# Routing of a mixture of experts: token places listed on chip during the routing stage, results stored at fixed rows and gathered by place

## The chip, the cores and the metric

The kernel runs on one core of a Trainium2 chip. The time is the device time of one launch, in microseconds (us), from the first to the last instruction with what lies around it. Three runs of the kernel before gave 2531.51, 2540.93 and 2547.09 us; the median is 2540.93.

## The reference, cut to what matters

A decoder layer on x [8, 100, 1024]: self attention, cross attention over 722 context rows, and a mixture of 64 experts of which each token takes 8. The change is in the third part, where B = 8 batches of S = 100 tokens make 800 tokens and 6400 (token, expert) pairs:

```python
router_logits = x2d @ gate_w                                  # [800, 64]
routing_weights = softmax(router_logits)
routing_weights, selected_experts = top_k(routing_weights, 8)
routing_weights = routing_weights / sum(routing_weights)
flat_sel = selected_experts.reshape(-1)
sorted_sel = argsort(flat_sel); token_idx = sorted_sel // 8
sorted_inputs = take(x2d, token_idx)                          # rows, expert by expert, bf16
w0 = ragged_dot(sorted_inputs, gate); w1 = ragged_dot(sorted_inputs, up)   # 1024 -> 384
expert_out = ragged_dot(silu(w0) * w1, down)                  # 384 -> 1024
out[t] = sum_k weight[t, k] * expert_out[row of (t, k)]
```

## The kernel before, in words

`decoder_kernel` runs seven stages one after the other: `self_attention_phase`, `query_phase`, `cross_image_phase`, `cross_text_phase`, `route_phase`, `experts_phase` and `combine_phase`. Each stage is a block: its engines run their own instruction lists, ordered by semaphores, and no engine begins the next stage until all have ended this one. So a stage lasts as long as its slowest engine list, waits for its own DMAs included.

**Casting ahead.** `Precast` copies the experts' f32 weights to bf16 in DRAM, 192 transfers on POOL's queue, two in flight, spread over the first four stages.

**Blanking.** In `self_attention_phase` POOL's list ends with 72 such casts and then 19 transfers of 1.5 MB of zeros over the rows of `results_d` (L242), one at a time: each waits for the one before to land, and the list ends with a wait for the last. Results that no tile of an expert ever writes are zeros by this. The other engines' work ends with the output projection: PE (L83), DVE's sum with the residual (L350), SP's store of x1 (L219).

**Routing stage** (`route_phase`). Per batch b PE projects the attention output (two halves of 24 matmuls, L81 to L83), DVE adds x1 (L1646), takes statistics and writes the normed rows `xn` (L1664), PE turns them (L1739) and multiplies by the gate (L1745), ACT copies out the logits (L1704). PE's order is project(b+1), router(b). POOL adds the bias to x1 (L1614) and stores `xn` as bf16 rows in DRAM (L1620). At the end SP waits for the casts and loads the first three experts' weights.

**Experts stage** (`experts_phase`). It starts with the choice of experts for all batches at once on DVE (`route`, L2004 to L2033: exp, top 8, marks, places from two matmuls), a table of tile counts and starts (`tabulate`), and for each expert a comparison of [100, 8 x 256] places with the marks (`seat_rows`, L2087) whose result PE multiplies by token numbers (`number_rows`, L2224, 32 matmuls of one column): this gives the numbers of the expert's tokens, which DVE casts to an index (L2101) and POOL uses to gather 128 rows of 2 KB (L1951). Then, in a loop over the 64 experts unrolled by four, step e of PE is: turn the rows of e+1 (L2245), the products of e with gate and up (L2253, 48 matmuls), the narrow product of e-1 (L2261), the numbers for e+4 (L2224). Experts with over 128 tokens run `further`: a tile more of the whole sequence with nothing beside it (L2293, L2253, L2261). The tile's indices come with the first gather; only a third tile needs new ones. Weights are held in four slots; SP loads e+3 (2304 KB, L1929) once the narrow product of e-1 has freed the slot. ACT stores results of 128 rows (256 KB, L2192) at a row that it loads from the table (`first_tile`). In the last steps DVE works out each token's result rows and weights (`find_results`, `find_weights`, `order_weights`, L2056 to L2083).

**Combining stage** (`combine_phase`). POOL gathers, for each batch and each of 8 choices, 100 rows of 2 KB by index (L2358, 64 gathers); DVE (5 of 8) and PE (3 of 8) weigh and add them.

Of the kernel before, what the change touches and what calls it, by code (L numbers as in the profile page):

```python
# [85 lines left out]
def self_attention_phase(nc, sems, cast, x_d, w_d, x1_d, clear_d):  # L86
# [9 lines left out]
    CLEARS = 19  # L96
    X_SLOTS, R_SLOTS = 4, 4
    with ExitStack() as ctx:
# [4 lines left out]
        zeros = sc.sb("zeros", [P, D], BF16)  # L103
# [38 lines left out]
        cleared, made, blanked = sc.sem("cleared"), sc.sem("made"), sc.sem("blanked")  # L142
# [81 lines left out]
        def _(pool):  # L224
# [7 lines left out]
            pool.memset(zeros[:, :], 0.0).then_inc(cleared, 1)  # L232
# [3 lines left out]

            blank = clear_d.rearrange("(c n p) d -> c p n d", p=P, c=CLEARS)
            pool.wait_ge(cleared, 3)
            for c in range(CLEARS):

                wait(pool, blanked, 16 * c)
                pool.dma_start(blank[c], zeros[:, :].unsqueeze(1).broadcast_to(blank[c].shape)  # L242
                               ).then_inc(blanked, 16)
            pool.wait_ge(blanked, 16 * CLEARS)

# [1261 lines left out]
MAX_TILES = ROWS // P + EXPERTS  # L1507
MATS, MAT = 3, KT * FF


class Routing:


    def __init__(self, sc):
        self.x2 = sc.sb("x2", [S, B, D])
        self.logits = sc.sb("logits", [S, B, EXPERTS])
        self.weights = sc.sb("weights", [S, B, TOP_K])
        self.results = sc.sb("results", [S, B * TOP_K], I32)


        self.table = sc.sb("table", [1, 4, EXPERTS], I32)

# [5 lines left out]
TILES, FIRST, FURTHER, THIRD = range(4)  # L1528


def route_phase(nc, sems, r, cast, x1_d, attn_d, w_out_d, b_out_d, gate_d, xn_d):

    with ExitStack() as ctx:
# [8 lines left out]
        at_raw = sc.sb("at_raw", [P, 2, KT, S])  # L1542
# [7 lines left out]
        std = sc.sb("std", [S, 2])  # L1550
        outp = sc.ps("outp", [P, 2, BANK])
        turn = sc.ps("turn", [P, 2, BANK])
        logit_ps = sc.ps("logit_ps", [P, BANK])

# [8 lines left out]
        outp_ready, x2_ready, x2_seen = sc.sem("outp_ready"), sc.sem("x2_ready"), sc.sem("x2_seen")  # L1563
        stats_done, stats_seen, var_ready = sc.sem("stats_done"), sc.sem("stats_seen"), sc.sem("var_ready")
        std_ready, rstd_ready, xn_ready = sc.sem("std_ready"), sc.sem("rstd_ready"), sc.sem("xn_ready")
        sent, send_step = [sc.sem(f"sent{u}") for u in range(2)], sc.sem("send_step")
        turned, xnT_ready = sc.sem("turned"), sc.sem("xnT_ready")
        router_ready, logits_ready = sc.sem("router_ready"), sc.sem("logits_ready")
        block = ctx.enter_context(nc.Block())

        @block.sync
        def _(sp):
# [34 lines left out]
        def _(pool):  # L1607
# [20 lines left out]
            for u in range(2):  # L1628
                send(B - 2 + u, u)
# [896 lines left out]
```

## Time and profile before

| | |
|---|---|
| median of 3 runs | 2540.93 us (2531.51 to 2547.09) |
| profiled execution, span | 2527.7 us (it is given as a span alone; its own time is not shown) |
| PE busy | 2011.5 us, 80% |
| PE weight load busy | 1692.7 us, 67% |
| DVE busy | 1130.7 us, 45% |
| ACT busy | 646.6 us, 26% |
| POOL busy | 468.2 us, 19% |
| DMA | 518.81 MB, mean 205 GB/s |

The spans of the stages, by the first instruction of each: self attention 0 to 510.7, queries to 672.7, cross attention to 1677.4, routing to 1827.9, experts to 2423.0, combining to the end. A slice of the page's busy table is 63.2 us. "Idle before, released by" names what ended an engine's wait; "issue" is a wait for nothing that the profile shows, such as a branch or a fetch of instructions.

### The profile page before, as it was taken

What the parts mean: (1) busy time and instruction counts of PE and PEld (TensorE: products, weight loads), DVE (VectorE), ACT (ScalarE), POOL (GpSimd) and SP (SyncE); (2) the same over time, 40 slices, a digit from 0 to 9 for tenths busy, and PEclk for the clock granted to TensorE, in tenths of its full rate; (3) what the DMA queues carried; (4) which work ended last, traced back from release to release, by engine and by line L of the source; (5) the groups of instructions that cost most, each with busy time, mean ns of one, the idle gap of its engine ahead of it and who ended that gap; (6) DMA issues with size and microseconds to landing.
All of it is one profiled execution on the core that took longest, in us unless ns stands there. A gap on an engine that the chain in (4) does not pass through costs nothing. (4 is left out here: it accounts for less than half of the span.)

```text
span 2527.7 us, 48690 instructions
## 1 busy us (share of the span) xinstructions
PE 2011.5 (80%) x17744; PEld 1692.7 (67%) x17745; DVE 1130.7 (45%) x2122; ACT 646.6 (26%) x1391; POOL 468.2 (19%) x556
## 2 busy tenths in 40 slices
PE   5999886059298989999959899959857788877756
PEld 4999864037298978888758777736656666666622
DVE  4444510034233354444433566643365555554366
ACT  4333300033221234434321344431101111111112
POOL 0111101101000011111100111101133334332156
PEclk9999988569699989999979999979979999999965
DMA  7999997669987255555276587833459989898445
GB/s 183 214 215 222 218 239 253 235 187 228 268 215 159 78 121 137 121 129 129 66 190 162 150 198 184 191 108 81 163 181 366 353 314 416 335 373 343 176 147 161
DMA packets 148152, 518.81 MB, mean 205 GB/s; under 512 B 27154, under 2 KB 68114, under 8 KB 140858
## 3 DMA queue, kind: packets, MB, share of 16 engines
q0 software_dynamic: 31776, 215.85, 38.2%
q1 hardware_dynamic: 105162, 281.04, 30.7%
q10 hardware_dynamic: 11088, 20.19, 2.1%
q8 instruction: 84, 1.38, 0.2%
q14 instruction: 42, 0.34, 0.0%
HBM read 582.94 MB, written 236.06 MB: 324 GB/s over the span
## 5 line engine op out<-in xcount | busy, mean ns | idle before, releaser
L81 PE MATMUL img_acc<-img_ctx_hi,img_w_hi 128*128 128x258 f32 x1024 | 303.4, 296 | 51.4 <-DVE img_ctx_lo L1158 40.1
L82 PE MATMUL img_acc<-img_ctx_lo,img_w_hi 128*128 128x258 f32 x1024 | 295.0, 288 | 0.1
L83 PE MATMUL img_acc<-img_ctx_hi,img_w_lo 128*128 128x258 f32 x1024 | 294.7, 288 | 0.0
L1780 POOL DMA_DIRECT2D experts_bf_dram<-in_moe_dram x192 | 98.3, 512 | 871.7 <-DMA experts_bf_dram<-in_moe_dram 542.2
L81 PEld LDWEIGHTS img_acc<-img_ctx_hi,img_w_hi 128*128 128x128 f32 x1024 | 199.8, 195 | 76.1 <-issue 65.4
L1951 POOL DMA_INDIRECT moe_rows<-expert_rows_dram,moe_index x77 | 150.3, 1952 | 387.1 <-DVE moe_index L2101 382.6
L82 PEld LDWEIGHTS img_acc<-img_ctx_lo,img_w_hi 128*128 128x128 f32 x1024 | 199.9, 195 | 0.4 <-issue 0.4
L83 PEld LDWEIGHTS img_acc<-img_ctx_hi,img_w_lo 128*128 128x128 f32 x1024 | 200.0, 195 | 0.0
L81 PE MATMUL txt_acc<-txt_ctx_hi,txt_w_hi 128*128 128x320 f32 x512 | 169.5, 331 | 37.5 <-DVE txt_ctx_lo L1158 29.2
L82 PE MATMUL txt_acc<-txt_ctx_lo,txt_w_hi 128*128 128x320 f32 x512 | 161.8, 316 | 0.0
L83 PE MATMUL txt_acc<-txt_ctx_hi,txt_w_lo 128*128 128x320 f32 x512 | 161.7, 316 | 0.0
L2087 DVE TENSOR_TENSOR moe_seated<-moe_picked,moe_seat 100x2048 bf16<-100x2048 f32 x64 | 145.9, 2282 | 0.1
L81 PE MATMUL self_acc<-self_xnT_hi,self_w_hi 128*128 128x400 f32 x384 | 136.6, 356 | 2.1 <-DVE self_xnT_lo L271 2.1
L81 PEld LDWEIGHTS txt_acc<-txt_ctx_hi,txt_w_hi 128*128 128x128 f32 x512 | 99.2, 194 | 52.1 <-issue 39.1
L82 PE MATMUL self_acc<-self_xnT_lo,self_w_hi 128*128 128x400 f32 x384 | 133.1, 347 | 0.0
L83 PE MATMUL self_acc<-self_xnT_hi,self_w_lo 128*128 128x400 f32 x384 | 132.6, 345 | 0.0
L83 PEld LDWEIGHTS txt_acc<-txt_ctx_hi,txt_w_lo 128*128 128x128 f32 x512 | 99.6, 194 | 0.0
L82 PEld LDWEIGHTS txt_acc<-txt_ctx_lo,txt_w_hi 128*128 128x128 f32 x512 | 99.4, 194 | 0.0
L2423 PE MATMUL comb_acc<-comb_part,comb_diag 100*100 100x512 bf16 x144 | 60.9, 592 | 43.6 <-DMA comb_part<-expert_results_dram,routing_results 41.5
L1045 POOL TENSOR_TENSOR img_kT<-img_kT,img_norm 128x258 f32<-128x258 f32 x64 | 47.0, 735 | 258.7 <-DMA img_kT<-cross_k_dram 258.6
L2245 PE MATMUL moe_turn<-moe_ident,moe_rows 128*128 128x128 bf16 x512 | 45.7, 233 | 60.6 <-issue 30.8
L745 PE MATMUL query_x_turn<-query_ident,query_xn 100*128 100x100 f32 x64 | 8.2, 281 | 104.1 <-ACT query_xn L705 101.6
(321 smaller groups left out, 4332.9 us busy)
## 6 DMA issues: line engine op xcount, KB each, us to landing
experts_bf_dram<-in_moe_dram POOLq DMA_DIRECT2D x192, 768.0 KB, 8.5
routing_w<-experts_bf_dram SPq DMA_DIRECT2D x48, 2304.0 KB
moe_w_last<-experts_bf_dram SPq DMA_DIRECT2D x16, 2304.0 KB
expert_results_dram<-self_zeros POOLq DMA_DIRECT2D x19, 1536.0 KB
self_w_raw<-in_w_self_dram SPq DMA_DIRECT2D x32, 512.0 KB, 12.0
expert_results_dram<-moe_out ACTq DMA_DIRECT2D x64, 256.0 KB, 7.3
img_raw<-in_ctx_img_dram SPq DMA_DIRECT2D x8, 1032.0 KB, 6.3
cross_k_dram<-img_kT SPq DMA_DIRECT2D x64, 129.0 KB, 2.0
```

The source lines that it names most:

```text
L81: eng.matmul(out, w_hi, a_hi, start=first, stop=False)
L82: eng.matmul(out, w_hi, a_lo, start=False, stop=False)
L83: return eng.matmul(out, w_lo, a_hi, start=False, stop=last)
L745: mm = pe.transpose(dst[:, kt // (KT // 2), col:col + S], src[:, kt * P:(kt + 1) * P], ident[0:S, 0:S])
L1045: pool.tensor_tensor(k, k, m.norm[:, cols:cols + part.cols], ALU.mult).then_inc(s.k_ready, 1)
L1780: pool.dma_start(self.dst_d[n], self.src_d[n]).then_inc(self.done[u], 16)
L1951: pool.indirect_dma_start(out=dst, out_offset=None, in_=xn_d[:, :], in_offset=bass.IndirectOffsetOnAxis(ap=rows_of, axis=0)).then_inc(load ...
L2087: return dve.tensor_tensor(dst, picked[:, :, bass.ts(e, 1)].broadcast_to(shape), seat[:, 0:places].unsqueeze(1).broadcast_to(shape), ALU.i ...
L2245: mm = pe.transpose(turn[:, k, :], rows[:, c % W_SLOTS, 0, k::KT], ident[:, :])
L2423: mm = pe.matmul(acc[0:S, b % 2, h, :], diag[:, done % 2, p, :], part[:, k, h * BANK:(h + 1) * BANK], start=n == 0 and p == 0, stop=k == O ...
```

## The change

The blanking goes, with its tile `zeros`. The experts stage no longer works out token numbers: `route`, `tabulate`, `seat_rows`, `number_rows`, `find_results` and `order_weights` are gone from it. In their place the routing stage does this per batch, on DVE, PE and POOL beside the projection: `choose` (top 8, their numbers, the marks), `rank` (two small matmuls), `find_places` (each token's 8 places, expert x 896 + rank), and `scatter` (POOL writes each token's number to its 8 places in DRAM lists, 4 bytes a token, 100 tokens an instruction, 8 instructions a batch, spread over four lists so that four are in flight). At the end SP loads the four lists, DVE takes their minimum, PE turns it, and `r.token` holds for every expert and tile the 128 token numbers. Unlisted places hold 800, a row of zeros. Results go to row e x 896 + 128 j, and the combining stage gathers by the places. The routing loops are unrolled, `at_raw` now shares memory with `at_lo`, and the results in DRAM are declared as 512 int32 a row instead of 1024 bf16.

```diff
 # self_attention_phase, POOL
-            pool.memset(zeros[:, :], 0.0).then_inc(cleared, 1)
             pool.wait_ge(x_split, B // 2)
             cast.start_some(pool, *CASTS_SELF)
-            blank = clear_d.rearrange("(c n p) d -> c p n d", p=P, c=CLEARS)
-            for c in range(CLEARS):
-                wait(pool, blanked, 16 * c)
-                pool.dma_start(blank[c], zeros[:, :]...).then_inc(blanked, 16)
-            pool.wait_ge(blanked, 16 * CLEARS)
 # route_phase, SP
-                wait(sp, at_split, b - 1)
+                wait(sp, outp_ready, 2 * (b - 1))
                 sp.dma_start(at_raw[:, u], attn_rows[b]).then_inc(at_loaded[u], 16)
...
+            sp.wait_ge(router_ready, B)
+            for n in range(LISTS):
+                sp.wait_ge(listed[n], 16 * B * TOP_K // LISTS)
+                sp.dma_start(list_rows[:, n], list_d[n].rearrange(...)).then_inc(list_loaded, 16)
+            sp.wait_ge(list_loaded, 16 * LISTS)
 # route_phase, POOL
+            def scatter(b):
+                pool.wait_ge(places_ready, b + 1)
+                for k in range(TOP_K):
+                    wait(pool, listed[k % LISTS], 16 * (b * TOP_K // LISTS + k // LISTS))
+                    pool.sem_inc(scatter_step, 1)
+                    pool.indirect_dma_start(
+                        out=list_d[k % LISTS][:, :],
+                        out_offset=bass.IndirectOffsetOnAxis(ap=r.places[:, b, k:k + 1], axis=0),
+                        in_=numbers[:, b:b + 1], in_offset=None).then_inc(listed[k % LISTS], 16)
+            for b in range(B):
+                send(b, b % 2)
+                if b + 2 < B:
+                    add_bias(b + 2, b % 2)
+                if b > 0:
+                    scatter(b - 1)
+            scatter(B - 1)
 # route_phase, DVE
+            def choose(b, u):
+                dve.wait_ge(logits_ready, b + 1)
+                link(dve.max(r.top[:, b, :], logits[:, u, :]))
+                dve.max_index(which[:, :], r.top[:, b, :], logits[:, u, :])
+                link(dve.match_replace(rest[:, :], r.top[:, b, :], logits[:, u, :], SELECTED))
+                dve.tensor_tensor(chosen[:, u, :], rest[:, :], logits[:, u, :],
+                                  ALU.not_equal).then_inc(chosen_ready, 1)
+                link(dve.tensor_tensor(match[:, :, :], expert_no..., which..., ALU.is_equal))
+            def find_places(b, u):
+                dve.wait_ge(ranked, b + 1)
+                link(dve.tensor_tensor(place[:, :], rank_ps[0:S, 0:EXPERTS], place_start[:, :], ALU.add))
+                link(dve.tensor_tensor(so_far[:, :], so_far[:, :], chosen[:, u, :], ALU.add))
+                link(dve.tensor_tensor(match[:, :, :], match[:, :, :], place..., ALU.mult))
+                link(dve.tensor_reduce(place_of[:, :], match[:, :, :], AX.X, ALU.add))
+                dve.tensor_copy(r.places[:, b, :], place_of[:, :]).then_inc(places_ready, 1)
+            for b in range(B):
+                norm(b, b % 2)
+                if b + 2 < B:
+                    split_at(b + 2, b % 2)
+                if b > 1:
+                    find_places(b - 2, b % 2)
+                if b > 0:
+                    choose(b - 1, (b - 1) % 2)
+            find_places(B - 2, 0)
+            choose(B - 1, 1)
+            find_places(B - 1, 1)
+            tabulate()
+            dve.wait_ge(list_loaded, 16 * LISTS)
+            link(dve.tensor_tensor(least[:, :, :], list_rows[:, 0], list_rows[:, 1], ALU.min))
...                              # two more minima, then PE turns 7 pieces and DVE copies to r.token
 # route_phase, PE
+            def rank(b, u):
+                wait(pe, places_ready, b)
+                pe.wait_ge(chosen_ready, b + 1)
+                pe.matmul(rank_ps[0:S, 0:EXPERTS], ones[:, :], so_far[:, :], start=True, stop=False)
+                pe.matmul(rank_ps[0:S, 0:EXPERTS], before[:, :], chosen[:, u, :], ...)
+            for b in range(2, B):
+                project(b, b % 2)
+                router(b - 1, (b - 1) % 2)
+                rank(b - 2, b % 2)
             router(B - 1, 1)
+            rank(B - 2, 0)
+            rank(B - 1, 1)
 # experts_phase
-                note_rows(e + W_SLOTS - 1, c + W_SLOTS - 1)      # DVE: index from number_ps
-                seat_rows(e + W_SLOTS, c)                        # DVE: [100, 2048] comparison
+                note_token(e + W_SLOTS - 1, c + W_SLOTS - 1)     # DVE: two columns of r.token
-                pick_rows(e + W_SLOTS, c)                        # PE: 32 matmuls of one column
-                    with pe.If(j > 1):                           # PE, in a further tile
-                        pe.wait_ge(x_seated_ready, x + 1)
-                        number_rows(2, x_seated).then_inc(x_numbered, 1)
-                    with pe.Else():
-                        pe.sem_inc(x_numbered, 1)
-                if isinstance(e, int) and e == EXPERTS - W_SLOTS:
-                    find_results()
-                    find_weights()
-                elif isinstance(e, int) and EXPERTS - W_SLOTS < e < EXPERTS:
-                    order_weights(e - 1 - EXPERTS + W_SLOTS)
-                    first = first_tile(act, e - 2)
-                    act.dma_start(out_d[bass.ts(first, P), :], out[...]).then_inc(stored[...], 16)
+                    act.dma_start(results_d[bass.ds(e * PLACES + j * P, P), :], src.bitcast(I32))...
 # combine_phase, POOL
                     pool.indirect_dma_start(
-                        out=part[:, k, :], out_offset=None, in_=rows_d[0:MAX_TILES * P, :],
-                        in_offset=bass.IndirectOffsetOnAxis(ap=r.results[:, c:c + 1], axis=0)
+                        out=part[:, k, :].bitcast(I32), out_offset=None, in_=rows_d[:, :],
+                        in_offset=bass.IndirectOffsetOnAxis(ap=r.places[:, b, k:k + 1], axis=0)
```

## Rows read from the trace of the kernel before

**Rows 1.** Waits of 420 to 520 us: engine, line, releaser, total, times, longest.
```profile
DVE query_stats L631 <- DMA query_x_row<-x_dram: 95.7, 1, 95.7
```
**Rows 2.** Timeline, end of self attention: start, length, instruction, idle before and its releaser.
```profile
419.71 0.29 SPq L219 DMA_DIRECT2D x_dram<-self_xn  x1
...
502.29 0.83 POOL L242 DMA_DIRECT2D expert_results_dram<-self_zeros  x1 [5.72 <-DMA expert_results_dram<-self_zeros]
510.72 0.69 SPq L590 DMA_DIRECT2D query_x_row<-x_dram  x2
```
**Rows 3.** Windows: stretch, length; busy (count) of PE, PEld, DVE, ACT, POOL; clock, DMA, GB/s.
```profile
1713.00:1828.00 115.00, 105.57 (x554) 78.90 (x552) 36.25 (x63) 17.30 (x32) 19.05 (x15) 0.96 0.42 116
1867.00:2409.00 542.00, 424.39 (x6477) 356.87 (x6475) 280.67 (x368) 80.34 (x149) 167.32 (x119) 0.95 0.85 332
```
**Rows 4.** Timeline from the last normed rows to the first expert.
```profile
1821.13 0.81 DVE L1664 TENSOR_SCALAR route_xn<-routing_x,route_mean_var,route_std 100x1024 f32<-100x1024 f32 x1
1827.48 0.21 ACT L1704 COPY routing_logits<-route_logit_ps 100x64 f32<-100x64 f32 x1 [3.02 <-PE route_logit_ps L1745]
...
1848.43 2.20 POOL L1951 DMA_INDIRECT moe_rows<-expert_rows_dram,moe_index  x1 [18.47 <-DVE moe_index L2101]
1857.02 1.27 PE L2253 MATMUL moe_gate_ps<-moe_rowsT,routing_w 128*128 128x128 bf16 x10
```
**Rows 5.** Prices of like instructions: tile queries of comb_part, moe_rows, expert_rows_dram; line groups; timeline.
```profile
L2358 POOL DMA_INDIRECT comb_part<-expert_results_dram,routing_results x64: 985/1000/1975, 2424.2 to 2514.9; - x64
DMA to landing us min/median/max: 3.7/4.3/7.8
L1951 POOL DMA_INDIRECT moe_rows<-expert_rows_dram,moe_index x77: 949/2202/2236, 1848.4 to 2394.5; - x77
DMA to landing us min/median/max: 3.2/3.3/7.7
POOL comb_part L2358 <- issue: 19.2, 62, 0.6
1838.09 0.69 DVE L2033 TENSOR_TENSOR moe_picked<-moe_place,moe_chosen 100x512 f32<-100x512 f32 x1
```
**Rows 6.** Timeline, one step of an expert without a further tile.
```profile
2163.18 1.50 PE L2253 MATMUL moe_gate_ps<-moe_rowsT,routing_w 128*128 128x128 bf16 x24
2165.86 1.46 PE L2261 MATMUL moe_out_ps<-routing_w,moe_inner 128*128 128x512 bf16 x6
2167.16 0.94 PE L2224 MATMUL moe_number_ps<-moe_number,moe_seated 100*128 100x1 bf16 x32
2167.51 0.37 SPq L1929 DMA_DIRECT2D routing_w<-experts_bf_dram  x1
2168.64 0.71 PE L2245 MATMUL moe_turn<-moe_ident,moe_rows 128*128 128x128 bf16 x8 [0.54 <-issue]
2169.18 1.00 PE L2253 MATMUL moe_gate_ps<-moe_rowsT,routing_w 128*128 128x128 bf16 x15
```
**Rows 7.** DMA view: rate in 40 slices of 2080 to 2160; then issues by size.
```profile
GB/s 377 420 402 401 431 427 381 425 425 420 422 422 402 429 419 407 419 423 411 406 429 418 406 411 428 408 410 431 411 409 418 421 420 415 410 424 424 249 27 0
...
moe_w_last<-experts_bf_dram SPq DMA_DIRECT2D x16, 2304.0 KB
...
expert_results_dram<-moe_out ACTq DMA_DIRECT2D x64, 256.0 KB, 7.3
```
**Rows 8.** Waits in the loop, 1870 to 2400.
```profile
PE moe_turn L2293 <- issue: 25.5, 13, 2.0
```
**Rows 9.** Timeline, the end of the experts stage.
```profile
2396.88 0.38 SPq L1929 DMA_DIRECT2D moe_w_last<-experts_bf_dram  x1
2409.17 1.52 PE L2253 MATMUL moe_gate_ps<-moe_rowsT,moe_w_last 128*128 128x128 bf16 x24 [1.87 <-DMA moe_w_last<-experts_bf_dram]
...
2415.11 4.41 DVE L2083 TENSOR_REDUCE routing_weights<-moe_match 100x64 f32<-100x4096 f32 x1
2422.97 0.20 POOL L72 MEMSET comb_ident<- 128x128 bf16 x1 [26.89 <-POOLq L1820]
```

More of the change, by code:

```diff
@@ L1515, in __init__ @@
         self.x2 = sc.sb("x2", [S, B, D])
-        self.logits = sc.sb("logits", [S, B, EXPERTS])
+        self.top = sc.sb("top", [S, B, TOP_K])
         self.weights = sc.sb("weights", [S, B, TOP_K])
-        self.results = sc.sb("results", [S, B * TOP_K], I32)
-        self.table = sc.sb("table", [1, 4, EXPERTS], I32)
+        self.token = sc.sb("token", [P, MAX_TILES_OF, EXPERTS], I32)
+        self.places = sc.sb("places", [S, B, TOP_K], I32)
+        self.table = sc.sb("table", [1, 3, EXPERTS], I32)
         self.w = [sc.sb(f"w{e}", [P, MATS, MAT], BF16) for e in range(W_SLOTS - 1)]
@@ L1550, in route_phase @@
         std = sc.sb("std", [S, 2])
+        logits = sc.sb("logits", [S, 2, EXPERTS])
+        rest = sc.sb("rest", [S, EXPERTS])
+        chosen = sc.sb("chosen", [S, 2, EXPERTS], BF16)
+        so_far = sc.sb("so_far", [S, EXPERTS], BF16)
+        before = sc.sb("before", [S, S], BF16)
+        ones = sc.sb("ones", [S, S], BF16)
+        expert_int = sc.sb("expert_int", [S, EXPERTS], I32)
+        start_int = sc.sb("start_int", [S, EXPERTS], I32)
+        expert_no = sc.sb("expert_no", [S, EXPERTS])
+        place_start = sc.sb("place_start", [S, EXPERTS])
+        which = sc.sb("which", [S, TOP_K], mybir.dt.uint32)
+        place = sc.sb("place", [S, EXPERTS])
+        place_of = sc.sb("place_of", [S, TOP_K])
+        numbers = sc.sb("numbers", [S, B], I32)
+        unit = sc.sb("unit", [1, EXPERTS])
+        tiles_of = sc.sb("tiles_of", [1, EXPERTS])
+        tile_end = sc.sb("tile_end", [1, EXPERTS])
+        behind = sc.sb("behind", [1, EXPERTS])
+        thirds_of = sc.sb("thirds_of", [1, EXPERTS])
+        third_end = sc.sb("third_end", [1, EXPERTS])
+        at_raw = at_lo[:, :, :, :].bitcast(F32)
+        match = w_raw[0:S, 1, 0:TOP_K * EXPERTS].rearrange("s (k e) -> s k e", k=TOP_K)
+        list_f = w_raw[0:EXPERTS, 1, 0:PLACES].rearrange("e (t p) -> e t p", p=P)
+        least = w_raw[0:EXPERTS, 0, 0:PLACES].bitcast(I32).rearrange("e (t p) -> e t p", p=P)
+        list_rows = w_hi[0:EXPERTS, 0:LISTS, 0:PLACES].bitcast(I32).rearrange("e n (t p) -> e n t p", p=P)
+        empty = xnT[:, :, :].rearrange("p k s -> p (k s)")[:, 0:EXPERTS * MAX_TILES_OF].bitcast(I32)
+        no_row = xn[0:1, 1, 0:D // 2].bitcast(BF16)
         outp = sc.ps("outp", [P, 2, BANK])
@@ L1595, in _ @@
                         load_x1(u, u)
[L1596 to L1599 removed]
+            for b in range(2, B):
+                load_at(b, b % 2)
+                load_x1(b, b % 2)
             for u in range(2):
@@ L1703, in collect @@
                 act.wait_ge(router_ready, b + 1)
-                act.copy(r.logits[:, b, :], logit_ps[0:S, 0:EXPERTS]).then_inc(logits_ready, 1)
+                wait(act, places_ready, b - 1)
+                act.copy(logits[:, u, :], logit_ps[0:S, 0:EXPERTS]).then_inc(logits_ready, 1)
             split_at(0, 0)
@@ L2171, in _, with store @@
             act.sem_inc(x_stored, 16)
-            act.wait_ge(centred, 1)
-            act.activation(r.logits[:, :, :], r.logits[:, :, :], ACT.Exp).then_inc(exp_ready, 1)
-            await_table(act)
+            act.wait_ge(shifted_ready, 1)
+            act.activation(shifted[:, :, :], shifted[:, :, :], ACT.Exp).then_inc(exp_ready, 1)
+            def store(e, j, src, done):
+                row = bass.ds(e * PLACES + j * P, P)
+                act.dma_start(results_d[row, :], src.bitcast(I32)).then_inc(done, 16)
             def step(g, c):
```

394 lines of the change are left out of this document (141 added, 253 removed).

## The prediction

> **What bounds the kernel now.** Every stage ends with its slowest engine list, so I read, stage by stage, which list ends last.
>
> The waits between 420 and 520 us come first: DVE stands 95.7 us for the first row of the query stage [rows 1]. The timeline of that stretch says why. SP issues the last store of self attention at 419.7; after that only POOL goes on, with its blanks, the last issued at 502.3, and the query stage starts at 510.7 [rows 2]. A blank takes 6.6 us (5.72 waited, 0.83 issued), so the last lands near 508.9, and the change of stage costs 1.8 us. Nothing else runs: this is 90 us of blanking in the open.
>
> The windows come next [rows 3]. Eight batches of routing take 115 us, 14.4 each, with PE busy 105.6: PE sets it. DVE is busy 36.3 us of it (4.5 a batch), POOL 19.1. From the last logits at 1827.5 to the first expert product at 1857.0 lies the choice on DVE, 29.5 us, with the first gather issued at 1848.4, 8.6 us before the products [rows 4].
>
> The loop over the experts is bound twice. A plain step takes 6.0 us, gate to gate, on PE: gate and up, the narrow product ending 4.14 after the gate's start, the numbers ending at 4.92, a gap of 0.54, the turn [rows 6]. But the DMA stands at about 417 GB/s in long plain stretches, and a step moves 2304 KB of weights, 256 KB of gathered rows and 256 KB of results [rows 7], 2.88 MB or 6.9 us. The loop as a whole moves 332 GB/s over 542 us [rows 3], 180 MB, which is 431 us at 417 GB/s: 111 us are spare, because the 13 further tiles [rows 8] leave the queue idle.
>
> **The change, part by part**
>
> *Blanking gone.* The store at 419.7 needs 0.3 us and a landing of about 2.3; a store of rows from POOL lands in 3.3 [rows 5]. With 1.8 us for the change of stage the queries start at 424 instead of 510.7: **-87 us**. The casts, which come before the blanks on POOL's queue, are done by then. Bounds -84 to -90.
>
> *Routing, beside the projection.* DVE gains per batch three or four passes over 512 elements at 0.69 us [rows 5] and nine small ones at about 0.2, with their links 4 us, on top of 4.5 in 14.4: hidden, and the next batch's first sum comes a microsecond later at most, while PE needs it 5 us after. PE gains two small matmuls a batch and a wait, 0.4 us, in the open: +3. The later load of `at_raw` lands before PE's turn comes, 7 us later: 0. POOL gains 64 scatters, which the trace doesn't show. The nearest rows are the 64 gathers of the combining stage: 1.0 us and a gap of 0.3 each, landing in 4.3 [rows 5]; with four lists in flight the landing allows one per 1.3 us too. So I take 1.3 us. A batch costs POOL 8 x 1.3 + 3.0 for its old work, 13.4 of 14.4 us: it just keeps up. Upper bound: the gathers of the experts stage, 2.2 + 0.3 = 2.5 us [rows 5].
>
> Those 2.2 us against 1.0 are 1.2 us more for a gather issued while DVE compares [100, 2048] for 2.28 us; in the combining stage no such pass runs. The new passes last 0.7 us [rows 5], and three of them fall beside the last 24 scatters: at most 2 us, which I add below. The Trainium skill ("SBUF — State Buffer", Who interferes with whom) has the rule behind it: a DVE instruction with two SBUF inputs and a GpSimd instruction that reads SBUF keep each other out for their whole length. By that rule, the trace agrees, and it speaks against putting both on these engines side by side; without it the sum would be 2 us less.
>
> *Routing, the tail.* The last batches pile up. Normed rows 7 are ready at 1821.9 [rows 4]; only then does DVE find the places of batch 5 (2.5 us), and POOL has 24 scatters, one store and 2 us of holding before it: 1824.4 + 31.2 + 0.6 + 2 = 1858.2. Landing 3.3: 1861.5. Loading the last list 4.4: 1865.9. Three minima over 896 elements, at the rate of the 0.69 us pass 1.2 each, 3.6; seven turns with a cold PE 2.6; the copy 0.6: 1872.7. Change of stage and first gather 1.5: 1874.2. Then 8.6 as before [rows 4], 1.0 less as the gathers aren't held by DVE, 1.5 more as the fourth expert's weights are now requested in the same microsecond; with PE's 3 from above: 1886.3. Before 1857.0: **+29 us**. Bounds: +15, if POOL is ahead and its last 16 scatters alone stand; +103, if all 64 cost 2.5 us (1.2 x 62 more).
>
> *The loop.* A plain step loses the numbers: narrow ends at 4.14, then gap and turn, 5.2 instead of 6.0 [rows 6]. That is 0.78 x 60 = 47, and a further tile loses a branch and a comparison's wait, 0.4 of the 2.0 us before its turn [rows 8], 5 in all: 52 us if nothing else binds. The DMA does. At 5.2 us a step asks for 6.9 us of transfers, and a load needs 12.3 us from issue to use when it is late (2396.9 to 2409.2 [rows 9]), while the distance from issue (4.33 after a gate [rows 6]) to the gate three steps on shrinks from 13.7 to 11.3. So plain stretches run at the DMA's 6.9, less what the tile before let it get ahead. Each tile gives some 9 us of lead, each plain step eats 1.7: stretches of up to five steps stay free, the two long ones of about ten steps give back 8 each, the rest a few: 18 in all. **-34 us**. Bounds -52 (no DMA limit) and -15 (the spare 111 us can't be moved to where they are missed). DVE loses 2.28 us a step and ACT a register load: both were hidden.
>
> *End of the stage.* DVE's last reduction of 4.4 us over the pairs and the copy behind it ended the stage at 2423.0 [rows 9]; the last load's landing at 2409.2 holds the last product in either kernel. From it: 2.8 products, 2.9 for two narrow products, copy, store and change 5: 2419.5. **-4 us**.
>
> *Combining.* The same 64 gathers of 2 KB rows, the chain of DVE, PE and POOL unchanged; rows now lie over 117 MB. 0, bounds -4 to +6.
>
> Sum: -87 + 29 - 34 - 4 = **-96 us**. The profiled span of 2527.7 becomes 2432. The median of the runs lies 13.2 us above that span, the fastest 3.8, and which run was profiled isn't shown; I carry the 13.2: **2445 us**.
>
> **The rivals**
>
> *A, the scatters are expensive.* All the gain rests on 64 transfers of 100 x 4 bytes, and the chain is serial: POOL starts them at about 1754, so each microsecond per scatter is 64 us on the end. It decides from 1.3 + 96/64 = 2.8 us each: above it the kernel is slower than before. With landings of 11 us on four lists that would be so, and the worst landing of a gather was 7.8 [rows 5]. At 2.5 us each: 2445 + 74 = 2519, no change; at 3.5 us: 2445 + 141 = 2586, slower. The Trainium skill ("DMA: Bandwidth & Descriptors", Specifications) says that a transfer under 512 bytes is done by the engine as read, modify and write; no row here shows what such a write costs. For it: 4-byte writes at random rows, nothing like it in the trace. Against: seven of them per DMA engine and scatter.
>
> *B, the loop gets it all.* PE's step falls to under 5.2 and the DMA gets ahead in the tiles' 111 us: loop -52, 2427.
>
> *C, the DMA keeps the loop.* Loop -15: 2464.
>
> *D, the routing tail is longer than counted* by POOL being behind at batch 5 (13.4 of 14.4 leaves nothing): 1.8 us a scatter, +32: 2477.
>
> *E, the blanking was not the end of its stage*: another list would end late in its place. The rows show no one after 420 [rows 2]; 2530.
>
> **How the numbers follow.** Forecast 0.50 (2420 to 2462 by itself); B 0.12; C 0.10; D 0.16; A at about 2.5 us 0.05, A slower 0.04; E 0.03. The range takes in B, C and D and half of the runs' spread: 2408 to 2490, with 0.15 outside. A measurement here tells 1%, 25 us, from no change. Faster by over that: 0.50 + 0.12 + 0.10 + 0.16 = 0.88, and 0.02 of A's weaker half, 0.90; within 0.06; slower 0.04.
>
> **What would show it.** The query stage starts near 424, its first DVE wait gone. POOL's 64 scatters start 1.3 us apart and keep up with the batches until the sixth; the first product comes some 56 us after the last logits instead of 29.5. Gate to gate 5.2 us behind a further tile and 6.9 at the end of long plain stretches, with waits for weights where before PE had hardly any. The combining stage keeps its 104 us. The forecast fails if the first product comes over 100 us after the last logits, or the DMA in the loop stays at 332 GB/s.

## The result

The kernel after takes 2412.99 us (median of 3 runs, 2411.33 to 2416.94) against 2540.93: ratio 0.9515, 95% interval 0.948 to 0.955. The forecast was 2445 us with a range of 2408 to 2490, so direction and range held, and the gain was a third larger than forecast (128 us against 96). The profiled execution's span fell from 2527.7 to 2409.9 us, by 117.8. So of the 32 us by which the forecast was too high, 22 lie in the stages; the other 10 come from the 13.2 us that were carried from the profiled span to the median, where the kernel after has 3.1.

Where the 117.8 us came from, stage by stage (each stage runs to the first instruction of the next; the experts stage is cut at its first product and at the last silu of the loop):

| stretch | before | after | difference | forecast (0 also where it named no term) |
|---|---|---|---|---|
| self attention | 510.8 | 426.0 | -84.8 | -87 |
| queries | 161.9 | 162.5 | +0.6 | 0 |
| image attention | 591.8 | 584.2 | -7.6 | 0 |
| text attention | 412.9 | 413.0 | +0.1 | 0 |
| routing, to the first expert product | 179.6 | 207.8 | +28.2 | +29 |
| first product to last silu | 553.7 | 500.0 | -53.7 | -34 |
| last silu to combining | 12.3 | 8.5 | -3.8 | -4 |
| combining | 104.7 | 107.9 | +3.2 | 0 |

All but one of the terms that were forecast came out within 4 us. The loop gave 20 us more. The image stage's 7.6 us are in code that did not change: over the 14 profiled executions of this study it lasted 583.7 to 593.3 us, in both kernels' code, so they, and the 3.2 us of combining (103.3 to 111.7), are what one execution differs from another by.

### The profile page after: what moved, and what is told of

Read it like the earlier page. It is cut to its first block and busy times, and to the rows that moved or that the text cites. A ratio compares the mean times of both kernels' runs of the same rounds, so it can differ in the third digit from the quotient of the medians.

```text
span 2409.9 us, 44056 instructions
## 1 busy us (share of the span) xinstructions
PE 1952.7 (81%) x15718; PEld 1635.6 (68%) x15719; DVE 1001.9 (42%) x2092; ACT 643.1 (27%) x1389; POOL 448.4 (19%) x606
## 5 line engine op out<-in xcount | busy, mean ns | idle before, releaser
L2009 POOL DMA_INDIRECT moe_rows<-expert_rows_dram,moe_token x77 | 75.0, 975 | 387.1 <-DVE moe_token L2060 382.0
L2080 DVE TENSOR_TENSOR moe_inner<-moe_silu,moe_up_ps 128x384 bf16<-128x384 f32 x64 | 35.5, 554 | 157.7 <-ACT moe_silu L2142 86.7
L2190 PE MATMUL moe_gate_ps<-moe_rowsT,routing_w 128*128 128x128 bf16 x1152 | 80.8, 232 | 18.9 <-DMA routing_w<-experts_bf_dram 15.3
L2183 PEld LDWEIGHTS moe_turn<-moe_ident,moe_rows 128*128 128x128 bf16 x512 | 41.1, 149 | 76.5 <-issue 68.9
## 6 DMA issues: line engine op xcount, KB each, us to landing
routing_w<-experts_bf_dram SPq DMA_DIRECT2D x48, 2304.0 KB, 15.3
```

The lines of the kernel that those rows point to most:

```text
L2009: pool.indirect_dma_start(out=dst, out_offset=None, in_=xn_d[:, :], in_offset=bass.IndirectOffsetOnAxis(ap=rows_of, axis=0)).then_inc(load ...
L2080: dve.tensor_tensor(inner[:, c % 2].rearrange("p f s -> p (f s)"), silu[:, c % 2], up_ps[:, c % 2, 0:FT * P], ALU.mult).then_inc(inner_rea ...
L2183: mm = pe.transpose(turn[:, k, :], rows[:, c % W_SLOTS, 0, k::KT], ident[:, :])
L2190: mm = pe.matmul(ps[:, u, f * P:(f + 1) * P], mat(slot, n, FF)[:, k, f::FT], x[:, k, :], start=k == 0, stop=k == KT - 1)
```

## The profile after

**The end of self attention** [rows 1, 2]: the timeline of SP and POOL.
```profile
417.39 5.84 SPq L217 DMA_DIRECT2D x_dram<-self_xn  x2
425.91 0.10 POOL L604 MEMSET query_ln_eps<- 128x1 f32 x1 [54.14 <-POOLq L97]
425.92 0.68 SPq L578 DMA_DIRECT2D query_x_row<-x_dram  x2
```
SP's last store is issued by 423.2, and the query stage starts 2.7 us later. DVE's wait of 95.7 us is gone; POOL has been done for 54 us.

**The routing stage** [rows 3, 4]. First the scatters and list loads as the tile query of the lists gives them (ns min/median/max, first and last start), then windows: the last seven batches, the tail behind the last places, the loop. Columns as in rows 3.
```profile
L1673 POOL DMA_INDIRECT expert_list_dram<-route_numbers,routing_places x64: 972/980/1676, 1664.0 to 1769.7; - x64
DMA to landing us min/median/max: 2.1/2.5/7.5
```
```profile
1640.00:1742.00 102.00, 88.44 (x499) 67.04 (x497) 61.05 (x147) 13.97 (x28) 60.05 (x53) 0.96 0.42 123
1742.00:1781.00 39.00, 1.27 (x8) 0.98 (x8) 7.80 (x22) 0.00 (x0) 22.18 (x23) 0.50 0.14 29
1794.00:2294.00 500.00, 384.52 (x4733) 315.93 (x4731) 150.80 (x288) 81.65 (x152) 98.69 (x122) 0.93 0.92 361
```
A scatter costs 0.98 us, 1.28 from start to start, as a gather of the combining stage does [rows 5]. In the tail of 39 us only POOL works for more than half of the time. The timeline shows the chain from the last places to the first product:
```profile
1737.16 0.21 ACT L1821 COPY route_logits<-route_logit_ps 100x64 f32<-100x64 f32 x1 [3.02 <-PE route_logit_ps L1859]
...
1742.94 0.17 DVE L1749 CAST routing_places<-route_place_of 100x8 int32<-100x8 f32 x1
...
1769.73 0.97 POOL L1673 DMA_INDIRECT expert_list_dram<-route_numbers,routing_places  x1 [0.30 <-issue]
1776.42 1.08 DVE L1792 TENSOR_TENSOR route_w_raw<-route_w_hi 64x896 int32<-64x896 int32 x1 [29.04 <-DMA route_w_hi<-expert_list_dram]
...
1780.83 0.62 DVE L1796 CAST routing_token<-route_list_ps 128x448 int32<-128x448 f32 x1 [1.10 <-PE route_list_ps L1889]
1781.72 0.37 SPq L2002 DMA_DIRECT2D moe_w_last<-experts_bf_dram  x1
...
1782.90 1.01 POOL L2009 DMA_INDIRECT moe_rows<-expert_rows_dram,moe_token  x1 [0.53 <-issue]
...
1790.73 1.05 PE L2183 MATMUL moe_turn<-moe_ident,moe_rows 128*128 128x128 bf16 x8 [9.93 <-DMA moe_rows<-expert_rows_dram]
...
1793.49 2.77 PE L2190 MATMUL moe_gate_ps<-moe_rowsT,routing_w 128*128 128x128 bf16 x24
...
1796.30 0.49 ACT L2142 ACTIVATE moe_silu<-moe_gate_ps 128x384 f32<-128x384 f32 x1 [11.64 <-PE moe_gate_ps L2190]
```
Places of the last batch are ready at 1742.9, POOL scatters until 1770.7. From the last logits to the first product it takes 56.3 us; "some 56 us" had been forecast.

**One plain step** of the loop, when nothing is late [rows 6]:
```profile
2067.38 1.50 PE L2190 MATMUL moe_gate_ps<-moe_rowsT,routing_w 128*128 128x128 bf16 x24
2068.72 1.50 PE L2190 MATMUL moe_up_ps<-moe_rowsT,routing_w 128*128 128x128 bf16 x24
2070.06 1.46 PE L2197 MATMUL moe_out_ps<-routing_w,moe_inner 128*128 128x512 bf16 x6
2071.36 0.65 PE L2183 MATMUL moe_turn<-moe_ident,moe_rows 128*128 128x128 bf16 x8
2071.84 1.50 PE L2190 MATMUL moe_gate_ps<-moe_rowsT,routing_w 128*128 128x128 bf16 x24
```
Gate to gate it is 4.46 us, not the 5.2 of the forecast: the turn follows the narrow product at once, and the gap of 0.54 us is gone with the 32 matmuls of one column.

**What PE waits for in the loop** [rows 8]: engine, tile and line, releaser, total, times, longest, 1794 to 2294.
```profile
PE moe_gate_ps L2190 <- DVE moe_x_rowsT L2098: 25.7, 13, 2.5
PE moe_turn L2183 <- DVE moe_x_out L2106: 18.2, 13, 1.7
PE moe_gate_ps L2190 <- DMA routing_w<-experts_bf_dram: 15.3, 10, 2.7
PE moe_turn L2183 <- DMA moe_rows<-expert_rows_dram,moe_token: 14.5, 6, 4.3
PE moe_gate_ps L2190 <- DMA moe_w_last<-experts_bf_dram: 9.9, 6, 2.8
PE moe_turn L2183 <- DMA moe_rows<-expert_rows_dram: 9.8, 6, 2.4
...
PE moe_turn L2223 <- POOLq L2037: 5.2, 7, 1.5
```
Weights hold PE for 25.2 us and gathered rows for 24.3. In the kernel before it was 5.9 and 9.8 us, and "issue" stood first; of the 25.5 us ahead of the 13 further tiles' turns [rows 8] 5.2 are left, spent on POOL. But the product behind that turn waits for DVE's copy of the turned rows, the longest entry here, and in the kernel before that wait was short:
```profile
PE moe_gate_ps L2253 <- DVE moe_x_rowsT L2142: 10.2, 13, 0.8
```
The two together went from 35.7 to 30.9 us, 0.4 us a further tile: the gap that PE lost came back as a wait for DVE, whose own idle time before that copy is now mostly put down to "issue" (15.0 us in ten of the 13).

**The steps one by one.** From silu to silu the loop has 63 steps, 13 of them with a further tile. Those 13 fell from 219.9 to 191.7 us (16.9 to 14.7 each), the 50 plain ones from 331.2 to 305.4 (6.62 to 6.11 each, where 4.46 is possible). In the last eight steps of the run of ten plain ones (1993.9 to 2050.0, before 2085.5 to 2141.3) nothing was gained: 56.1 us after and 55.7 before, 7.0 a step, at 414 and 416 GB/s. And behind a further tile only two plain steps are quick in the kernel after; the third takes 7.1 to 10.3 us, in each of the nine places that have one.

**The end of the experts stage** [rows 9]:
```profile
2279.00 0.38 SPq L2002 DMA_DIRECT2D moe_w_last<-experts_bf_dram  x1
...
2290.68 2.74 PE L2190 MATMUL moe_gate_ps<-moe_rowsT,moe_w_last 128*128 128x128 bf16 x24 [2.77 <-DMA moe_w_last<-experts_bf_dram]
...
2293.46 0.49 ACT L2142 ACTIVATE moe_silu<-moe_gate_ps 128x384 f32<-128x384 f32 x1 [4.93 <-PE moe_gate_ps L2190]
...
2302.01 0.20 POOL L72 MEMSET comb_ident<- 128x128 bf16 x1 [23.86 <-POOLq L1939]
```
The last weights' load still holds the last product, as forecast.

## The experiments

All in one table; "loop" is from the first to the last silu of the 64 experts, "routing" is the routing stage, both of the profiled execution. The kernel after was run a second time beside the last three (median 2421.51 us), so a difference of medians below some 10 us between sets of runs says nothing; the stages say more. Kernels whose loop is the one of the kernel after (after, after again, bias on DVE, blanks back, rank early) had loops of 497.2, 503.1, 498.6, 506.5 and 504.8: mean 502, spread 9.

| kernel | median us | ratio to before, interval | loop | routing |
|---|---|---|---|---|
| before | 2540.93 | 1 | 551.2 | 150.5 |
| after | 2412.99 | 0.9515, 0.948 to 0.955 | 497.2 | 196.0 |
| after again | 2421.51 | 0.9565, 0.9538 to 0.9591 | 503.1 | 199.1 |
| half of the scatters | 2402.6 | 0.9469, 0.944 to 0.9499 | 505.0 | 177.7 |
| bias on DVE | 2409.64 | 0.9497, 0.945 to 0.9544 | 498.6 | 192.1 |
| numbers on PE | 2459.24 | 0.9693, 0.9662 to 0.9725 | 543.3 | 196.1 |
| pass on DVE | 2431.4 | 0.9586, 0.9554 to 0.9618 | 508.1 | 195.9 |
| after, less weights | 2388.41 | 0.9436, 0.9397 to 0.9474 | 472.5 | 195.6 |
| before, less weights | 2542.73 | 1.0018, 0.9993 to 1.0044 | 564.4 | 150.2 |
| blanks back | 2509.76 | 0.9896, 0.9852 to 0.9941 | 506.5 | 196.5 |
| rank early | 2413.26 | 0.9532, 0.9494 to 0.9569 | 504.8 | 188.6 |
| gather ahead | 2409.99 | 0.9512, 0.948 to 0.9543 | 491.7 | 199.5 |
| all three | 2399.88 | 0.9503, 0.9461 to 0.9545 | 492.7 | 186.0 |
| ahead, less weights | 2365.01 | 0.9342, 0.9305 to 0.9378 | 450.0 | 196.2 |

**Blanks back.** The control for the largest term.
```diff
+            blank = clear_d.rearrange("(c n p) d -> c p n d", p=P, c=19)
+            for c in range(19):
+                wait(pool, blanked, 16 * c)
+                pool.dma_start(blank[c], zeros[...]...).then_inc(blanked, 16)
+            pool.wait_ge(blanked, 16 * 19)
```


> The kernel after, with the 19 transfers of zeros put back on POOL's list behind the casts of the first stage, 1.5 MB each, one at a time. Theory 1: they run alone, and the first stage ends 83 to 88 us later and nothing else changes: 2498 us. Rival (the 8 us that the image stage gained, with unchanged code, also come from the blanking): 92 to 96 us more, 2507 us. Rival 2 (most of it would be hidden): under 60 us.


The first stage lasts 513.2 us, 87.3 more than in the kernel after (without blanks it lasted 418.8 to 427.9 us in eleven profiles), and the image stage 586.2, as without blanks. Theory 1 holds in the stages; of the 97 us between the medians (88 beside the second run of the kernel after) the rest is spread, 9 us of it in the loop (506.5). The rival that ties the image stage to the blanks falls.

**Numbers on PE** and **pass on DVE**: which part of the removed work was the loop's gain?
```diff
 # numbers on PE: behind narrow(e - 1)
+                    for n in range(32):
+                        pe.matmul(number_ps[:, n // 16:n // 16 + 1], ident[0:S, :], ident[0:S, 0:1], ...)
 # pass on DVE: behind note_token
+                    wait(dve, seated_ready, e)
+                    dve.tensor_tensor(seated[:, :, :], seat[...], places[...], ALU.is_equal)   # [100, 2048]
```


> The kernel after, with 32 matmuls of one column on PE in each of the 64 steps again (their result is not used); DVE's comparison stays away. Theory 1: the loop gained because PE's plain step fell from 6.0 to 4.5 us (0.8 us of matmuls and 0.7 us of a wait for nothing that the profile shows behind them): with the matmuls the step is 6.0 us and the loop is back by 45 to 54 of its 54 us, 2462 us. Theory 1b: only the 0.8 us of matmuls comes back, the gap was that of the old loop: where the DMA is the bound it is hidden, 15 to 30 us, 2436 us. Rival 2: the gain came from DVE's comparison and the short gathers, PE's matmuls were hidden by the DMA: 0 to 8 us, 2417 us.

> The kernel after, with one comparison of 100 x 2048 elements on DVE in each of the 64 steps again (its result is not used); PE's matmuls stay away. Theory 1: DVE has room for its 2.3 us; the gathers on POOL last 2.2 us instead of 1.0 and nothing waits for them: 0 to 6 us more, 2416 us. Rival 2: the gathers are issued late and land late, PE waits for rows: 20 us more or above, 2435 us.


With the matmuls alone the loop is back at 543.3, 41 us of the 49 by which 551.2 stands above the mean of 502; theory 1, not 1b, a little below its 45 by that mean. One step of it, and its waits for "issue":
```profile
2043.23 1.50 PE L2191 MATMUL moe_up_ps<-moe_rowsT,routing_w 128*128 128x128 bf16 x24
2044.57 1.46 PE L2198 MATMUL moe_out_ps<-moe_w_last,moe_inner 128*128 128x512 bf16 x6
2045.86 0.94 PE L2220 MATMUL moe_number_ps<-moe_ident 100*128 100x1 bf16 x32
2047.35 0.71 PE L2184 MATMUL moe_turn<-moe_ident,moe_rows 128*128 128x128 bf16 x8 [0.55 <-issue]
```
```profile
PE moe_turn L2184 <- issue: 33.0, 46, 1.9
PE moe_turn L2228 <- issue: 20.1, 13, 1.8
```
The gap behind the numbers is back, at 0.55 us, and so are 1.5 us ahead of each further tile, which in this kernel has no branch or comparison more than the kernel after. So both come with the 32 short matmuls: they cost PE 1.5 us a plain step, of which the profile calls 0.9 busy. Ahead of a further tile their gap hides DVE's: the wait for its copy is back at 10.2 us in all, from 25.7.

The pass on DVE costs more than the 0 to 6 us that theory 1 gave it by the medians, 18 us beside the first run of the kernel after and 10 beside the second; in the loop it is 6 us above the mean of 502, less than the spread of 9. Its gathers:
```profile
L2013 POOL DMA_INDIRECT moe_rows<-expert_rows_dram,moe_token x77 | 151.7, 1970 | 329.5 <-DVE moe_token L2064 323.9 <-issue 5.5
```
1970 ns against 973, and PE waits for rows 47.6 us in the loop instead of 24.3, while its waits for weights fall from 25.2 to 12.5. So the pass makes rows later, but what it costs the loop is not clear of the spread; it is the smaller part.

**Less weights**, in either kernel: is the loop bound by bytes?
```diff
-                    sp.dma_start(w[slot][:, :, :], cast.of_expert(e)).then_inc(w_loaded[slot], 16)
+                    some = MATS if isinstance(e, int) and e < W_SLOTS else 2
+                    sp.dma_start(w[slot][:, 0:some, :], cast.of_expert(e)[:, 0:some, :]).then_inc(...)
```


> The kernel before, with the same cut of the weights' loads. Theory 1: the old loop was mostly bound by PE's 6.0 us: 50 x 6.0 + 13 x 16.8 = 518 us from first to last silu instead of 551, so 25 to 35 us less, 2510 us: what PE gained (1.5 us a plain step) is then worth about 108 us where no transfer binds, and 54 of it were lost to the DMA in the kernel after. Rival (the old loop was bound by the DMA as much as the new one): 70 us less, 2470 us.

> The kernel after, with the loads of the experts' weights cut to gate and up from the fifth expert on (1536 KB instead of 2304 KB; the narrow products use what an earlier expert left in the slot). Theory 1: in the new loop the DMA is the bound wherever PE is not in a further tile; with 2.1 MB a step it falls away, and all plain steps run at PE's 4.5 us: 50 x 4.5 + 13 x 14.2 = 410 us from the first to the last silu instead of 497, so 70 to 87 us less, 2335 us. Rival: PE, DVE and ACT bound the loop between them and the transfers are hidden: up to 10 us less, 2405 us.


Before: nothing in the time (ratio 1.0018), less than theory 1's 25 to 35 us. The last eight of the ten plain steps did get shorter, 51.7 us for 55.7, and no wait for weights is left; but the profiled execution, the slowest of its ten, had a lower granted clock in the loop (0.91 for 0.95) and further tiles of 17.6 us for 16.9. So bytes held the kernel before in that run, for some 4 us, and nothing shows that they did elsewhere. After: 30 us off the loop, between the theories (those eight steps take 43.6 us for 56.1); bytes bind the new loop, but with them gone PE still waits 24 us for rows, and does not reach its 4.5 us.

**Gather ahead**: the rows. In the kernel after, a load of weights, the gather of an expert's rows with the small transfer that follows it where there is no second tile, and the turn that needs them:
```profile
2067.24 0.37 SPq L2002 DMA_DIRECT2D moe_w_last<-experts_bf_dram  x1
...
2069.77 0.98 POOL L2009 DMA_INDIRECT moe_rows<-expert_rows_dram,moe_token  x1 [3.45 <-DVE moe_token L2060]
2070.82 0.56 POOL L2023 DMA_DIRECT2D moe_rows<-expert_rows_dram  x1
...
2078.37 1.07 PE L2183 MATMUL moe_turn<-moe_ident,moe_rows 128*128 128x128 bf16 x8 [2.39 <-DMA moe_rows<-expert_rows_dram]
2079.24 2.70 PE L2190 MATMUL moe_gate_ps<-moe_rowsT,moe_w_last 128*128 128x128 bf16 x24
```
The gather is called "three ahead", but it is issued 2.4 us behind the product's start at 2067.38, and at 4.46 us a step the turn that wants it would start at 2075.8, 6.1 us later; here it landed 8.6 us after its issue. The product behind the wait runs at the lower level of the clock (granted 0.51 in 2079.3 to 2081.8, the 1.2 GHz level, against 1.00 in 2069 to 2078) and takes 2.70 us instead of 1.50. The granted clock of the loop is 0.93, against 0.95 before.
```diff
-                gather(g, c + W_SLOTS - 1)                 # POOL: both tiles of e + 3
+                gather(g, c + W_SLOTS)                     # first 128 rows of e + 4
+                gather_second(g, c + W_SLOTS - 1)          # second 128 rows of e + 3
...
-                turn_rows(e + 1, c + 1)                    # DVE
-                note_token(e + W_SLOTS - 1, c + W_SLOTS - 1)
+                note_token(e + W_SLOTS, c + W_SLOTS)
+                turn_rows(e + 1, c + 1)
```


> The kernel after, unchanged, beside the next three on the same chip: 2413 us within 5 us by every theory; what it differs by is what runs of one program vary by.

> The kernel after, with the gather of an expert's first 128 rows issued four steps ahead instead of three and ahead of DVE's copy of the turned rows (the gather of the second 128 rows stays three ahead). Theory 1: in the new loop PE's step of 4.5 us has outrun the landing of the gathered rows (median 15.3 us from issue, behind the bytes of a weights load), and 24 us of waits for rows are in the loop, with the clock's fall behind the longest of them; a step earlier they vanish, but a part turns into waits for weights: 10 to 18 us less, 2399 us. Rival 1 (only the bytes bind): the waits for rows turn into waits for weights one for one, 0 to 4 us less, 2411 us. Rival 2 (one gather more in the queue delays the loads): 5 us more, 2418 us.

> The kernel after, with the gathers of first rows a step ahead and the weights' loads cut to gate and up from the fifth expert on (the narrow products use what an earlier expert left in the slot). With the cut alone the loop took 473 us from first to last silu. Theory 1: what was left beyond PE's 410 to 420 us were the rows' landings; with both out of the way the loop runs at 415 to 435 us, 2345 us. Rival (something else binds, such as the second rows' gathers, POOL's list or the clock behind a further tile): above 455 us, 2375 us or more.


The kernel after, run again, was 3.5 us outside of the 5 us that had been allowed. The landing of 15.3 us that the second expectation names is the one that the page gives for the loads of weights; of gathers the trace of the kernel after gives no landing, and in gather ahead they took 3.5 to 8.7 us, 6.6 in the median. Gather ahead took 11.5 us off the kernel after again (the intervals still touch) and 10 off the loop, the lower edge of theory 1. The third steps behind a further tile now take 5.7 to 9.6 us, for 7.1 to 10.3; the last eight of the ten plain steps keep their 56.1. PE waits 17 us for rows, for 24 and 23 in the two profiles of the kernel after, and 32.5 for weights, for 25 and 36: whether waits for rows turned into waits for weights can't be told from that spread. With both the gathers ahead and fewer bytes the loop is 450 us, 101 less than before; that is 15 above theory 1's range, and the rival's 455 isn't reached. What PE waits for then:
```profile
PE moe_gate_ps L2203 <- DVE moe_x_rowsT L2111: 27.0, 13, 2.5
PE moe_turn L2196 <- DVE moe_x_out L2119: 18.1, 13, 1.7
PE moe_turn L2196 <- DMA moe_rows<-expert_rows_dram,moe_token: 9.9, 5, 3.7
```
Rows and weights are down to 13 us together. What is left are the further tiles' waits for DVE, 54.5 us in all and 53.3 in the kernel after, further steps of 15.2 us instead of theory 1's 14.2, and 12 us of "issue"; most plain steps are at 4.5 us.

**Half of the scatters**, **bias on DVE**, **rank early**: the routing tail.
```diff
 # half of the scatters
-                for k in range(TOP_K):
+                for k in range(LISTS):
 # bias on DVE: behind choose(b - 1)
-                    add_bias(b + 2, b % 2)         # POOL, between send and scatter
+                    add_bias(b + 2, b % 2)         # DVE, 1.22 us
 # rank early (with the bias on DVE)
-                rank(b - 2, b % 2)                 # PE, behind router(b - 1)
+                    if h == 1 and b > 1:           # PE, in project(b), between its halves
+                        rank(b - 2, b % 2)
```


> The kernel after, with only the first four of a token's eight places scattered (32 scatters of 100 numbers instead of 64); the lists lack the other places, so half of the gathered rows are the row of zeros, and all else is unchanged. Theory 1: in the routing stage POOL is what ends last: its 64 scatters start 1.28 us apart, and the bias of a later batch, queued behind them, holds DVE and so the whole stage (one batch 8 us longer). With 32 scatters POOL waits for the places instead, the last places come about 8 us earlier, and four scatters of 1.28 us follow: the stage is 24 to 30 us shorter, 2386 us. Rival: the chain behind the last places (landing, list loads, minima) sets the end whatever POOL does: only four scatters fewer, 5 us, 2408 us.

> The kernel after, with the bias added to x1 by DVE instead of POOL, behind the choice of the batch before; nothing else. Theory 1 (POOL's list is the bound of the routing stage and its add holds DVE): POOL loses 2 us of some 13.5 a batch, no batch waits for a bias, and the last scatter follows the last places by 8 x 1.28 us plus what POOL still is behind: 15 to 25 us less, 2393 us. Rival 1 (the scatters alone hold POOL, the adds fit into their waits): 0 to 5 us less, 2410 us. Rival 2 (DVE becomes the bound of a batch with 1.2 us more): the batches lengthen from 14.4 us by up to a microsecond, 8 us more, 2421 us.

> The kernel after with the bias on DVE and with PE's two rank matmuls of batch b moved from behind the router of batch b+1 into the middle of the projection of batch b+2, so that DVE finds a batch's places directly behind choosing it. Theory 1: the routing stage ends with the scatters that are left when the places of batch 5 come, and these come only behind the norm of batch 7; found 8 us earlier, POOL works without a pause and the last scatter starts 12 to 16 us earlier than with the bias on DVE alone: routing stage 178 us instead of 196, 2394 us. Rival: DVE's wait for PE in the middle of its list delays the sums of the next half, the batches lengthen from 14.4 us, and the stage gains nothing: 2413 us.


Half of the scatters: the stage is 18 us shorter, less than theory 1 and far more than its rival. The last places do not come earlier (158.5 us into the stage, 157.2 in the kernel after), so the batch that the bias had held cost nothing at the end; what counts is POOL's backlog, 12 scatters instead of 24 behind the places of batch 5. (Of the 18 us the loop gave back 7.8 and the combining stage 3.8, each within its spread.) Bias on DVE: 4 us, rival 1; POOL, relieved, waited 27 us for places instead. Rank early gives 3.5 us more, not 12 to 16. Its POOL timeline shows why:
```profile
1730.08 0.62 POOL L1660 DMA_DIRECT2D expert_rows_dram<-route_xn  x1
1737.90 1.48 POOL L1668 DMA_INDIRECT expert_list_dram<-route_numbers,routing_places  x1 [7.20 <-DVE routing_places L1744]
...
1757.65 0.98 POOL L1668 DMA_INDIRECT expert_list_dram<-route_numbers,routing_places  x1 [0.30 <-issue]
```
POOL is through with batch 5 at 1730 and then stands 7.2 us for the places of batch 6, which still come behind the norm of batch 7; 16 scatters follow. The floor moved from 24 scatters to 16.

**All three**: the best version here.


> The kernel after, with the bias on DVE, PE's rank matmuls in the middle of the projection, and the gathers of first rows a step ahead. Theory 1: the routing stage gives 7 us as it did without the gathers' change, the loop its 10 to 18: 2391 us. Rival (the loop takes back what the routing stage gives, since the last weights' load binds): 2405 us.


2399.88 us against 2421.51 for the kernel after on the same chip, 21.6 less; the two intervals of the ratios still touch (0.9461 to 0.9545 and 0.9538 to 0.9591). Routing is 10 to 13 us shorter and the loop 4.5 to 10, where theory 1 had 7 and 10 to 18: more in the one, its lower edge or less in the other. The time is 9 us above its figure, as that of the kernel after is.

## Why the prediction was right, and where it was off

*Blanking, -87.* Right: 84.8 in the pair of profiles, 87.4 with the blanks put back.

*Routing beside the projection and its tail, +29.* Right at 28.2, and by the steps that were named: 1.28 us a scatter for 1.3, and 24 scatters from batch 5 on behind its places. That the list of tokens was ready 195.8 us into the stage for 195.3 is in part luck, since two sizes were off and cancelled. The last scatter ended 185.0 us into the stage for 180.8: POOL did not keep up until the sixth batch but was 4.5 to 7.7 us behind the places from the third on (4.8 at batch 5), and its waits for landings (the longest took 7.5 us), 6.9 us in seven, four of them over a microsecond and the last of those at 1719.8, are part of that. Against it the tail of landing, loading and turning the lists was shorter, 10.7 us from the last scatter to the copy's end for 14.5; no row had shown the 4.4 us for loading a list, and landing and load took 5.7 together for 3.3 + 4.4. From the first gather's issue to the first product it was 10.6 us for 9.1, the gather landing 7.8 us after its issue, beside the weights' load of a microsecond earlier. The 3 us for `rank` were more than it took: the last logits came 151.4 us into the stage for 150.0 before. Rival A had its break-even at 2.8 us a scatter: nothing came near. The Trainium skill ("DMA: Bandwidth & Descriptors", Specifications) has transfers under 512 bytes done as read, modify and write; these 4-byte ones landed in 2.1 to 7.5 us, no later than the combining stage's gathers of 2 KB rows (3.7 to 7.8 [rows 5]), so here the rule is not seen to cost anything. (The landings of 3.2 to 7.7 us in rows 5 are those of the stores of normed rows; for the gathers printed above them the trace has none.)

*The loop, -34.* The direction and the mechanism held: PE's step shorter, then the queue as the limit. In the last eight of the ten plain steps the limit is the forecast's own, 7.0 us a step at 414 GB/s for 6.9 at 417. Two sizes were off, one on each side. The first is in "a plain step loses the numbers: narrow ends at 4.14, then gap and turn, 5.2 instead of 6.0": the gap was taken for a property of the turn, and it came with the numbers. The step is 4.46 us. A step with a further tile lost 2.2 us where 1.2 had been counted (0.78 and 0.4): 0.9 are the numbers, the 0.4 ahead of its turn were right (35.7 to 30.9 us in 13), and some 0.7 are its gate and up products, which took 4.2 us together before and 3.5 after, nearer to the 3.0 that they take at the upper level of the clock; no run shows why. PE alone could so give 50 x 1.5 + 13 x 2.2 = 103 us where 52 had been counted (an estimate from these steps).

The second is what the DMA takes back, 18 us in the forecast and some 50 by that estimate. "Each tile gives some 9 us of lead" and "stretches of up to five steps stay free" did not hold: the third plain step behind a tile already takes 7.1 to 10.3 us. With a step of 4.46 a load of weights has 9 us from its issue to the gate that needs it (3 x 4.46 - 4.33), not 11.3, and it lands later, after 15.3 us in the median by the page:
```profile
routing_w<-experts_bf_dram SPq DMA_DIRECT2D x48, 2304.0 KB, 15.3
```
Rows later than the weights had been no part of the forecast. Gather ahead and less weights together gave 52 us back, all of it in the plain steps (252.9 us). So the two errors cancelled in part, 103 - 49 for 52 - 18, which is luck. So is it that rival B's -52 is what was measured, 49 to 54: its PE step of 5.2 us and its idle queue are not what the traces show.

The reading that the loop before was "bound twice" was right for the run of ten plain steps, where the kernel before needs the same 7.0 us a step and less weights shortened it, and wrong for the loop as a whole: with its transfers cut by a quarter the time did not change. A DMA share of 0.85 [rows 3] and stretches at 417 GB/s did not mean that PE waited for them much; the waits for weights and rows, 15.7 us in all, said so.

*DVE's pass.* That it was "hidden" in the kernel before was not tested; put into the new loop it costs 6 us there, within the spread, and 10 to 18 by the medians. The Trainium skill ("SBUF — State Buffer", Who interferes with whom) has DVE passes with two SBUF inputs and GpSimd's reads exclude each other; the gathers of 1970 ns beside the pass and 973 without it agree.

*End of the stage -4, combining 0.* Right at -3.8, and at 3.2 within the spread.

## What to carry to other kernels

Read a gap that follows a row of very short matmuls as a part of their price, and test it by adding them elsewhere. Look, too, at what stands right behind a wait that goes: another engine's delay may have run beside it, and takes its place. When PE's step gets shorter, every transfer that was started a fixed number of steps ahead gets less time in the same measure: recount the distance in microseconds for the small gathers, too, not for the largest load alone. A queue that is 85% busy on average can bind one stretch and leave the rest alone: compare the same steps of both kernels one by one.

## What was not expected of the hardware

32 matmuls of one column, each with its own load of weights, cost PE 1.5 us (47 ns each), with 0.94 us shown as busy and 0.55 as a wait for nothing shown; ahead of a further tile that gap was 1.5 us, but there DVE's delay ran beside it. A scatter of 100 x 4 bytes costs POOL 0.98 us, hardly less than a gather of 100 x 2 KB (1.00 before, 1.04 after, the medians). And some waits of PE cost more than themselves: behind one of 2.39 us the next 24 products took 2.70 us instead of 1.50 (granted clock 0.51), behind one of 2.77 us 2.74 (granted 0.50, 2290.8 to 2293.2), while behind another of 2.38 us they took 1.52.
